# Two attention streams of one batch each become one stream of 16 head pairs, with a new preparation in front

## What is computed

```python
q = _split_heads(x @ Wq + bq, h)
k = _split_heads(x @ Wk + bk, h)
v = _split_heads(x @ Wv + bv, h)
pattern = jnp.einsum('bhid,bhjd->bhij', k, q) * scale
prob = jax.nn.softmax(pattern, axis=-2)
out = jnp.einsum('bhis,bhid->bhsd', prob, v)
concat = out.transpose(0, 2, 1, 3).reshape(b, s, h * dv)
return concat @ Wo + bo
```

## Time and profile before

| | us |
|---|---|
| median of 3 runs | 5114.24 (5112.64 to 5126.45) |
| the profiled execution, time | 5104.81 |
| its span | 5103.0 |
| mean granted clock of TensorE | 0.959 |

### The profile page before, as it was taken

How to read it: one execution, slowest core, us unless ns; L and a number is a source line. 1 busy time by engine, 2 the same in 40 slices (tenths; PEclk the granted TensorE clock), 3 DMA queues, 4 the chain that set the end, 5 groups by cost and what they waited for, 6 DMA issues and landing times.

```text
span 5103.0 us, 64759 instructions
## 1 busy us (share of the span) xinstructions
PE 4646.0 (91%) x21552; PEld 2817.8 (55%) x21552; DVE 3551.9 (70%) x4520; ACT 2193.0 (43%) x3447; POOL 2726.0 (53%) x1142
## 2 busy tenths in 40 slices
PE   5899999999999689999999999975989897999898
PEld 3455555555554245555555555534767675777576
DVE  4888888888786578878878778755556454556445
ACT  2344444444443234444444444333655443655442
POOL 0456656656666236666566566543666322666422
PEclk8899999999999789999999999997999998999898
DMA  1000000000000000000000000010000100000000
GB/s 41 5 4 2 5 4 2 5 4 2 5 1 2 20 5 4 2 6 1 5 6 1 6 5 1 2 37 17 1 1 1 35 1 17 1 1 1 0 1 33
DMA packets 57187, 37.21 MB, mean 7 GB/s; under 512 B 32972, under 2 KB 55456, under 8 KB 56864
## 3 DMA queue, kind: packets, MB, share of 16 engines
q1 hardware_dynamic: 56864, 33.02, 2.2%
HBM read 28.54 MB, written 4.19 MB: 6 GB/s over the span
## 4 chain that ended last, share of the span: by engine, by line
POOL 46%; issue 28%; PE 13%; DVE 8%; ACT 3%; POOLq 1%; DMA 1%; DVEq 0%; SPq 0%; ACTq 0%
POOL accp L639 35%; PE psum L1480 4%; POOL lp L661 4%; PE psum L1355 3%; POOL accp L635 3%; POOL rnorm L651 2%; POOL qk_u L656 2%; DVE ssq L1025 1%; ACT lp L785 1%; PE psum L1401 1%; DVE lnr L393 1%; ACT qk_sq L769 1%; PE psum L1493 1%; DVE lnc L398 1%; DVE qk_w L1037 1%
## 5 line engine op out<-in xcount | busy, mean ns | idle before, releaser
L639 POOL TENSOR_TENSOR accp<-accp,prob 128x1024 f32<-128x1024 f32 x640 | 1635.7, 2556 | 699.8 <-ACT prob L733 659.5
L733 ACT ACTIVATE prob<-psum 128x1024 f32<-128x1024 f32 x1024 | 1038.5, 1024 | 1669.5 <-PE psum L1258 1527.6
L922 DVE TENSOR_REDUCE mx<-psum 128x1 f32<-128x512 f32 x1920 | 1230.9, 683 | 382.6 <-PE psum L1235 351.0
L1269 PE MATMUL psum<-prob,vv 128*64 128x512 f32 x4096 | 991.9, 605 | 0.0
L1257 PE MATMUL psum<-qhh,klh 128*128 128x512 f32 x2048 | 837.3, 409 | 32.8 <-DVE klh L910 13.0
L1258 PE MATMUL psum<-qlm,kh 65*128 65x512 f32 x2048 | 823.7, 402 | 0.0
L1235 PE MATMUL psum<-klh,qhh 128*128 128x512 f32 x1920 | 699.8, 423 | 53.9 <-DVE mx L922 51.5
L1235 PEld LDWEIGHTS psum<-klh,qhh 128*128 128x128 f32 x1920 | 339.6, 191 | 448.8 <-DVE mx L922 309.7
L1269 PEld LDWEIGHTS psum<-prob,vv 128*64 128x64 f32 x4096 | 248.7, 136 | 509.9 <-issue 368.7
L1257 PEld LDWEIGHTS psum<-qhh,klh 128*128 128x128 f32 x2048 | 396.1, 193 | 211.7 <-issue 85.1
L639 POOL TENSOR_TENSOR accp<-prob 128x1024 f32<-128x1024 f32 x64 | 154.9, 2421 | 668.8 <-ACT prob L733 663.7
(11 more groups left out here) (152 smaller groups left out, 6725.2 us busy)
## 6 DMA issues: line engine op xcount, KB each, us to landing
tok<-L_attn_x SPq DMA_DIRECT2D x32, 128.0 KB, 2.2
rot_l<-const_rot SPq DMA_DIRECT2D x2, 2048.0 KB, 9.3
out<-lpT SPq DMA_DIRECT2D x32, 128.0 KB, 1.7
wqkv_l<-L_ffn_wqkv SPq DMA_DIRECT2D x4, 768.0 KB, 10.6
w_l<-L_ffn_w SPq DMA_DIRECT2D x4, 682.0 KB
wqk<-L_attn_Wq SPq DMA_DIRECT2D x32, 64.0 KB, 2.1
wqk<-L_attn_Wk SPq DMA_DIRECT2D x32, 64.0 KB, 2.2
wv_p<-L_attn_Wv SPq DMA_DIRECT2D x16, 128.0 KB, 2.3
```

Source lines behind the costliest of these rows:

```text
L639: pool.tensor_tensor(acc_p[cp][:], first[:], prob[kt % PRING][:], ALU.add).then_inc(pool_sum, 1)
L733: act.activation(prob[t % PRING][:], psum[:, S_BANK + 2 * (t % 2):S_BANK + 2 * (t % 2) + 2, :].rearrange("p a b -> p (a b)"), ACT.Exp, sca ...
L922: dve.tensor_reduce(mx4[:, j // CHUNKS, j % CHUNKS:j % CHUNKS + 1], ps, AX_X, ALU.max).then_inc(ring_free, 1)
L1269: mm = pe.matmul(psum[j * DH:(j + 1) * DH, O_BANK, :], vv[:, kt, s * DH:(s + 1) * DH], prob[t % PRING][:, j * T:(j + 1) * T], start=(kt == ...
```

## The change

The attention of both batches becomes one stream of 16 pairs (ALL_PAIRS). Pair 7 is the new BRIDGE: its heads carry maxima and projections of batch 1's first heads, and in groups 5 to 12 of its first head eight items turn_h. Each turns two token tiles of batch 1's normed input (four transposes) and VectorE writes them, scaled and shifted, over hT. The weights of the groups of turn_h in max_places become 3, those of groups 11 and 12 too. The six phases in front of layer norm 2 become one; pair 8 is a MIDDLE pair, written out on VectorE and SyncE and in the loop on TensorE.

Layer norm 1 works on token-major tiles, in quads of four: sum, centred squares, variance, power -0.5, one operation per tile; then the turn, and scale and shift at the read of PSUM. For batch 0, VectorE takes the sums and ScalarE the squares. For batch 1, ScalarE takes both (next_statistics) and GpSimd normalises into h_next, which the bridge reads.

The first head's maxima run in 32 couples of 512-column products. Between them stand on TensorE (ASIDE): from couple 1 on the second head's projections, the values, the bias product, and the 16 turns of the input into xT, read by ScalarE with gabo as bias. All loads of both batches' x are issued at the start, batch 1's behind the first weights and Wo.

```diff
-RING_PRO = V_ITEMS + RING_MAX + 1
+ALL_PAIRS = B * PAIRS
+COUPLES = RING_MAX // 2
+QUADS = KT // 4
+TWINS = KT // 2
+BRIDGE_PLACES = TWINS + 1
 ATT_SCALE = 1.0 / np.sqrt(np.float32(DH))
...
+        def quad(t):
+            return t[:].rearrange("p (t d) -> p t d", d=D)
+        x_quads = [[quad(t) for t in acc_p + acc_d],
+                   [x_tail[:, 4 * q:4 * q + 4, :] for q in range(3)] + [x_last[:]]]
+        h_quads = [[quad(t) for t in prob], [h_next[:, 4 * q:4 * q + 4, :] for q in range(QUADS)]]
+        wo_all = oT[:].rearrange("p (k n) -> p k n", n=D)
...
+            turns = range(TURN_GROUP, TURN_GROUP + TWINS) if which == BRIDGE and hh == 0 else ()
+            placed = max_places([*outs, *turns])
...
+        def places(kind, j, hh):
+            if kind == "turn":
+                return TURN_PLACES[hh]
+            if kind == "turn_h":
+                return 2 if j == TWINS - 1 else 1
...
+        ASIDE = {}
+        for n, item in enumerate([("qk", i) for i in range(QK_ITEMS)] + [("v", i) for i in range(V_ITEMS)]
+                                 + [("bo", i) for i in range(4)] + [("x", k) for k in range(2 * TWINS)]):
+            ASIDE.setdefault(1 + n, []).append(item)
+        P1_READ = (3, 4, 5, 6)
...
+            sp.dma_start(identf[:], eye).then_inc(id_in, 16)
+            for h in range(HALVES):
+                sp.dma_start(csil[:, h, :], c_in[:, h * P:(h + 1) * P].rearrange("b p -> p b")).then_inc(c_raw, 16)
+            sp.dma_start(wmod_sb, wmod.rearrange("(h p) n -> p h n", p=P)).then_inc(wm_in, 16)
+            for q in range(QUADS):
+                sp.dma_start(x_quads[0][q], x[0, q * T:(q + 1) * T, :].rearrange("(t p) d -> p t d", p=P)).then_inc(x0_in[q], 16)
...
+            load_head(0, 0)
+            load_head(1, 1)
+            load_wv(0)
+            sp.dma_start(bo_t[:], bo.rearrange("(m p) -> p m", p=P)).then_inc(bo_in, 16)
+            sp.dma_start(bv_t[:], bv.rearrange("(m p) -> p m", p=P)).then_inc(bo_in, 16)
+            sp.dma_start(wo_all, Wo.rearrange("(k p) n -> p k n", p=P)).then_inc(bo_in, 16)
+            for q in range(QUADS):
+                sp.dma_start(x_quads[1][q], x[1, q * T:(q + 1) * T, :].rearrange("(t p) d -> p t d", p=P)).then_inc(x1_in, 16)
             sp.sem_inc(mrow, 16)
-            for b in range(B):
...
+            pair(PAIRS - 1, False, PAIRS - 1, 0, BRIDGE)
+            pair(PAIRS, True, 0, 1, MIDDLE)
+            with sp.Fori(1, PAIRS - 1) as hp:
+                pair(hp + PAIRS, True, hp, hp + 1, MIDDLE)
+            pair(ALL_PAIRS - 1, True, PAIRS - 1, None, LAST)
...
+            for q in range(QUADS):
+                pool.wait_ge(var_ok, q + 1)
+                inverse_deviation(0, q)
+            for q in range(QUADS):
+                at = slice(4 * q, 4 * q + 4)
+                pool.wait_ge(sq1_ok, 4 * (q + 1))
+                pool.tensor_scalar(st_var[:, 1, at], st_ssq[:, 1, at], 1.0 / D, EPS, ALU.mult, ALU.add).then_inc(var1_ok, 1)
+                pool.wait_ge(var1_ok, q + 1)
+                inverse_deviation(1, q)
+                pool.wait_ge(rs1_ok, q + 1)
+                for t in range(4):
+                    i = 4 * q + t
+                    op = pool.tensor_scalar(h_quads[1][q][:, t, :], x_quads[1][q][:, t, :], st_neg[:, 1, i:i + 1], st_rs[:, 1, i:i + 1], ALU.add, ALU.mult)
+                op.then_inc(h1_ok, 1)
...
+            def next_statistics(q):
+                if q == 0:
+                    act.wait_ge(x1_in, 16 * QUADS)
+                for t in range(4):
+                    i = 4 * q + t
+                    if i >= 2:
+                        act.wait_ge(neg1_ok, i - 1)
+                    act.activation(copies[:, i % 2, :], x_quads[1][q][:, t, :], ACT.Copy, scale=-1.0 / D, accum_out=st_neg[:, 1, i:i + 1]).then_inc(neg1_ok, 1)
+                act.wait_ge(neg1_ok, 4 * (q + 1))
+                centred_squares(1, q)
...
+            def read_input(k):
+                act.wait_ge(xt_full, k + 1)
+                b, i = divmod(k, TWINS)
+                for h in range(HALVES):
+                    op = act.activation(xT[:, b, h, i * D:(i + 1) * D], psum[:, 1 + k % 3, h * D:(h + 1) * D], ACT.Identity, bias=gabo[:, b, h:h + 1])
+                op.then_inc(xt_ok, 1)
+            for q in range(QUADS):
+                act.wait_ge(neg_ok, q + 1)
+                centred_squares(0, q)
+            next_statistics(0)
+            next_statistics(1)
+            act.wait_ge(su_d, 3)
+            for q in range(QUADS):
+                act.wait_ge(ht_full, HALVES * q + 2)
+                act.activation(hT[:, 1, q * T:(q + 1) * T], psum[:, HALVES * (q % 2) + 1, :], ACT.Identity, bias=mod[:, 1, 0:1], scale=mod[:, 3, 0:1]).then_inc(ht_act, 1)
+            project(0, 0, 4)
+            project(1, 1)
+            for i in range(V_ITEMS):
+                act.wait_ge(vv_full, i + 1)
+                act.activation(vv[:, i * V_TILES:(i + 1) * V_TILES, :], psum[:, i, :].rearrange("p (t d) -> p t d", d=P), ACT.Copy).then_inc(vv_ok, 1)
+            act.wait_ge(gabo_ok, B)
+            for k in range(TWINS):
+                read_input(k)
+            next_statistics(2)
+            next_statistics(3)
+            for k in range(TWINS, 2 * TWINS):
+                read_input(k)
...
+            for q in range(QUADS):
+                means(q)
+            variances(0)
+            variances(1)
+            normal(0)
+            variances(2)
+            normal(1)
+            variances(3)
+            normal(2)
+            normal(3)
...
+            for q in range(QUADS):
+                dve.wait_ge(ht_full, HALVES * q + 1)
+                dve.tensor_scalar(hT[:, 0, q * T:(q + 1) * T], psum[:, HALVES * (q % 2), :], mod[:, 2, 0:1], mod[:, 0, 0:1], ALU.mult, ALU.add).then_inc(ht_dve, 1)
...
+            def out_bias():
+                dve.wait_ge(bo_full, 1)
+                dve.tensor_tensor(bo_all[:], psum[:, 0, 0:HALVES], bo_t[:], ALU.add).then_inc(su_d, 1)
+                dve.wait_ge(su_d, 8)
+                for b in range(B):
+                    dve.tensor_tensor(gabo[:, b, :], mod[:, 4:6, b:b + 1].rearrange("p k o -> p (k o)"), bo_all[:], ALU.mult).then_inc(gabo_ok, 1)
+            for i in range(QK_ITEMS):
+                proj_qk(0, 0, i, 4)
+            for k in range(COUPLES):
+                dve.wait_ge(pm_full, k + 1)
+                qt, c = divmod(2 * k, CHUNKS)
+                at = 4 + 2 * (k % 2)
+                dve.tensor_reduce(mx4[:, qt, c:c + 2], psum[:, at:at + 2, :], AX_X, ALU.max).then_inc(pm_free, 1)
+                if k in P1_READ:
+                    proj_qk(1, 1, P1_READ.index(k))
+                if k == BO_READ:
+                    out_bias()
+            dve.wait_ge(pm_free, COUPLES)
+            dve.tensor_reduce(mx1[:], mx4[:], AX_X, ALU.max).then_inc(mx_red, 1)
...
+            def next_hidden(rb, r, i, count):
+                ps = ring_wait(rb, r)
                 for h in range(HALVES):
...
+                    op = dve.tensor_scalar(hT[:, h, i * D:(i + 1) * D], ps[:, h * D:(h + 1) * D], mod[:, 2 + h, 1:2], mod[:, h, 1:2], ALU.mult, ALU.add)
+                op.then_inc(ring_free, count)
...
+            with dve.Fori(1, PAIRS - 1) as p:
+                pair(p, False, 0, MIDDLE)
+            pair(PAIRS - 1, False, 0, BRIDGE)
+            pair(PAIRS, True, 0, MIDDLE)
+            with dve.Fori(PAIRS + 1, ALL_PAIRS - 1) as p:
+                pair(p, True, 1, MIDDLE)
+            pair(ALL_PAIRS - 1, True, 1, LAST)
...
+            def turn_next(rb, r, i, count):
+                ring_slot(rb, r)
+                if i == 0:
+                    pe.wait_ge(h1_ok, QUADS)
+                turn_twin(M_BANK + r % RING, twin(h_quads[1], i)).then_inc(ring_full, count)
...
+            def first_maxima(k):
+                if k >= 2:
+                    pe.wait_ge(pm_free, k - 1)
+                qt, c = divmod(2 * k, CHUNKS)
+                for j in range(2):
+                    mm = pe.matmul(psum[:, 4 + 2 * (k % 2) + j, :], qhh[0][:, qt * P:(qt + 1) * P], klh[0][:, (c + j) * T:(c + j + 1) * T],
+                                   start=True, stop=True)
+                mm.then_inc(pm_full, 1)
...
+            def turn_input(k):
+                b, i = divmod(k, TWINS)
+                if k < 3:
+                    pe.wait_ge(vv_ok, k + 2)
+                else:
+                    pe.wait_ge(xt_ok, k - 2)
+                if k == TWINS:
+                    pe.wait_ge(x1_in, 16 * QUADS)
+                turn_twin(1 + k % 3, twin(x_quads[b], i)).then_inc(xt_full, 1)
+            for q in range(3):
+                turn_hidden(q)
+            hidden(0)
+            proj_qk(0, 0, 0, 1, 4)
+            turn_hidden(3)
+            for q in range(1, QUADS):
+                hidden(q)
+                proj_qk(0, 0, q, 1, 4)
+            projected(0, QK_ITEMS)
+            for k in range(COUPLES):
+                first_maxima(k)
+                for kind, j in ASIDE.get(k, ()):
```

(76 more changed lines are left out.)

654 lines of the change are left out of this document (305 added, 349 removed).

## The result

The changed kernel takes 4971.64 us (median of 4 runs, 4963.63 to 4978.41), before stands at 5116.68 beside it; the ratio is 0.9724, with a 95% interval of 0.9710 to 0.9739. Forecast were 4965 us, 4935 to 5005. The sum of the prediction was made for one profiled execution and gave 4955.8 us; that of the changed kernel took 4973.04 (span 4971.3), 17.2 more. So the size came out, but two errors of opposite sign lie in it: the start gained 13.5 us more than forecast, the stream of pairs 31.0 less.

What follows compares the result with a forecast made beforehand. TensorE was taken to set the pace of the pairs, with relays where no engine is full. Start 36.4 plus stream 112.6 gave 149.0 us off the 5114.2 median: 4965 us, range 4935 to 5005.

Steps and rivals of the forecast that it cites:

- Step 2: Start: ScalarE's sixteen squares with sums at 0.69 us each end at 22.8 us; transposes start at 26.5.
- Step 3: Start: ScalarE waits for batch 1's x until about 26 us, then 11.1 us of statistics to 37.1, delaying hT.
- Step 4: Start: turns, reads and first projection products alternate to about 44 us; projected at about 54.
- Step 5 and 6: Start: 32 couples of maxima, sum 58.8 us, plus an 8.9 us TensorE stall from ScalarE's statistics amid input reads.
- Step 7: Start: turn and store of the maxima 3.1 us as before; first scores at about 124.8 us.
- The rival of a cold preparation: Start: lower clock level holds through the new stage, first scores at 150, total 4990 us; chance 15%.
- The gap: Between the two batches' streams: batch 1's load, norm, projections and stand-alone maxima leave the path, 130.3 us removed.
- crowding: Bridge, groups 11 and 12: extra maxima and turn_h where VectorE has no room; 4 us TensorE stall, bounds 0 and 7.
- The seams: Pairs 8 and 9 after the bridge: 196.4 us (0 to 4.9 extra) and 199.3 us as first passes of loops.
- I count a boundary of VectorE's loops at 4 us: Where VectorE leaves a head-pair loop, the oT multiplications span 5.37 us against 1.39; 4 us added to pair 7.
- The rival "slower": Stream: first-pass price of 4.9 us at both heads of 15 pairs, 147 us; time say 5135 us; chance 2%.
- a disturbance: Batch 1's old stream: 1556.8 us measured against 1552.4 summed; 4.4 us that batch 0 lacks.

Runs made afterwards that it cites:

- the repeat: The changed kernel run once more with nothing edited: 4978.67 us, ratio 0.9731 to the kernel before.
- other places: Changed kernel with 73 or 32 empty instructions ahead of TensorE's first wait: 4955.67 us (ratio 0.9685) and 4975.8 us (0.9726).
- the fastest kernel: Changed kernel plus batch 1's statistics moved later, GpSimd's first addition per head waiting for VectorE's oT products, and 32 empty instructions: 4865.42 us, ratio 0.9507.
- GpSimd's wait: GpSimd's first addition of each head waits for VectorE's oT products of the head before: changed kernel 4917.5 us; kernel before, with it alone, 5047.3 us.

## Why the prediction came out

**The start** (forecast first scores at 124.8, measured 111.34). The order of the chain was right, and its sizes too large. Step 2: squares at 0.49 us, not 0.69; transposes at 23.5, not 26.5. Step 3: x of batch 1 landed at 27.6 (forecast 26), but statistics took 7.4 us, not 11.1. Step 4: projected at 51.8, not 54. Step 5 and 6: 56.9 us up to the turn of the maxima instead of 67.7, of which the stall is 4.95 instead of 8.9. The rest is in the couples: 3 to 6 took 9.2 us instead of 12.6, 7 to 12 took 11.7 instead of 13.5 (a part of the output bias 0.95 us instead of 1.7), 13 to 28 without the stall 19.4 instead of 22.4; those up to couple 2 gave some of it back, partly at the low clock. Step 7: 2.65 instead of 3.1. The 13.5 us are 2.2, 10.8 and 0.5. The late pieces that I named, ScalarE's half of hT and the input reads, were the ones; moving the statistics took these away. The rival of a cold preparation did not come: the maxima stage held a granted clock of 0.91.

**The gap** of 130.3 us went and did not come back: there is no stretch without scores between pair 7 and pair 8.

**The bridge** (forecast 206.8, measured 204.5, and 204.5 to 210.3 in the repeat and at other places). The transposes can be read directly. Each of the eight items takes 0.53 us of TensorE, up to the start of the next product, and one at the low clock 1.04; the eight sum to 4.75 us:

```profile
1538.28 0.60 PE L1348 MATMUL psum<-identf,h_next 128*128 128x128 f32 x4
1538.81 1.94 PE L1440 MATMUL psum<-prob,vv 128*64 128x512 f32 x8
```

With the fastest kernel the other terms can be estimated. A straight pair without collisions takes 190.9 us; a loop pair of before, 194.4, is that, one collision of 2.3 (194.4 against 192.1) and 1.2 for the turn. The bridge of the fastest kernel takes 197.5: transposes 4.7 (forecast 4.4) and crowding 1.9 (forecast 4). The 7.0 us up to 204.5 I put down to the two collisions; less the 2.3 and 1.2 that a loop pair has, 3.5 are left for the start (forecast 4). 194.4 + 4.7 + 1.9 + 3.5 = 204.5. Of these only the 4.7 is measured by itself: in three other kernels with GpSimd's wait the bridge took 199.5 to 200.8 us, with more of it at the low clock or one more wait of 1.1 us, so the split is good to 2 or 3 us. The page's rule that I weighed (the Trainium skill, "TensorE: Matmul & The Clock Gate", "Part 4: PE-mode transpose", 275 ns each) would, as an estimate, have made it 8.8 us for the transposes; the rows show 0.13 us each. On its other half, that transposes do not count as activity for the clock, no run here decides: the maxima stage held 0.91, but with products between the transposes.

**The seams.** Pair 8 was forecast at 196.4 and took 200.7: TensorE reaches its start without a turn, and the multiplications collided there too (5.61 us). Pair 9 was forecast at 199.3 and took 195.9: TensorE paused at the turn, so GpSimd came later and nothing collided. The step that failed here is "I count a boundary of VectorE's loops at 4 us". Its size was about right and its mechanism wrong: it is a collision of GpSimd's addition with VectorE's multiplications, and TensorE's pause at a loop's turn happens to avoid it. Hence the other reading that I missed: the 4.80 us and the wait of 2.62 us stood in the middle of every pair but the last of each stream, in the price of 194.4 us that I took as TensorE's own.

**The loop pairs** are the term that was mis-sized: "pairs 2 to 6 ... 972.0" took 996.4, and two of them, 200.9 and 201.4, passed the bound of 200 that I had set as a sign of being wrong. The same instructions cost 4.9 us a pair more, through a second pause of 1.25 us and the low clock behind it, since the loop lies at another place of TensorE's stream. The rival "slower" spoke of such a price at both heads of 15 pairs, 147 us; it came at one head of five pairs. The trace of before, with its one place, could not tell it; why one place brings a second pause stays open.

Pairs 10 to 13 took 6.0 us more than forecast: 12 and 13 took some 197.4 us each, with the granted clock at 0.50 for 3 to 7 us behind TensorE's 2.6 us waits in their middles, and in pair 12 also behind the turn. In the kernel before, two pairs of batch 1's loop took 197.7 and 197.5 us in just this way. They make the 4.4 us that the prediction called a disturbance and left out (6.2 in the loop, less 1.8 in the last pair); with GpSimd's wait in the kernel before, these two took 192.0 and 193.7. Why the clock falls behind these waits and not behind the others stays open.

So the forecast was right in its main mechanism, the gap and the relay at the start, and in its time, but partly because 13.5 us more gained at the start stand against 31.0 less in the stream; the terms of the stream add up as 24.4 (pairs 2 to 6), −2.3 (bridge), 4.3 and −3.4 (pairs 8 and 9), 7.7 (pairs 10 to 15) and 0.3 (pairs 0 and 1).

## What to carry to other kernels

When an instruction has two durations in one trace, look first at what the other engines do in the same microsecond, before giving the longer one to the control flow around it; here one wait on an engine with 10 us to spare was worth half as much as the whole rewrite. A pair's price "in its loop" can hold a stall in its middle: read the waits of one steady iteration too, not only those that distinguish it from the others. And a loop moved to another place of the same instruction stream may change its price by some 2%, so a forecast of a rewrite should carry that as a term, and two versions should be compared at more than one place.

## What the runs showed of the hardware

**GpSimd's additions hold up VectorE's multiplications.** Two products of 64x512 with both inputs in SBUF take 1.39 us alone and 4.8 to 5.6 us when a GpSimd addition of 128x1024 (2.38 us) has just begun and a second follows at once. At 1501 us in the changed kernel they began at 1501.22 and took 5.52; GpSimd's additions ran from 1501.05 to 1503.43 and from 1503.77 to 1506.19, and by my estimate 2 x 0.69 for the products and two blocked stretches, of 2.2 and some 2 us, make it up. Where the second addition comes later there is one such stretch, 3.2 to 3.8 us in all, at the first sum inside the heads (in all but one of them, the bridge's first, where GpSimd came late):

```profile
1465.12 3.23 DVE L1110 TENSOR_TENSOR oT<-o_raw,rcp 64x512 f32<-64x512 f32 x2
...
1464.71 2.38 POOL L709 TENSOR_TENSOR accp<-accp,prob 128x1024 f32<-128x1024 f32 x1 [0.75 <-ACT prob L848]
...
1467.94 2.63 POOL L709 TENSOR_TENSOR accp<-accp,prob 128x1024 f32<-128x1024 f32 x1 [0.85 <-ACT prob L848]
```

TensorE has no wait there, no maxima being placed in that group, and GpSimd's wait leaves these as they are. The Trainium skill, "SBUF — State Buffer", "Who interferes with whom", says that a VectorE instruction with two SBUF inputs contends with a GpSimd instruction that reads SBUF, and that the shared port pair is an exclusive lock; of VectorE's two-port modes it says that whoever issues first has the pair for its whole instruction and the other is blocked. The trace agrees, with these numbers, and shows the blocking for this plain multiplication too.

**A turn of a loop costs TensorE a pause of 1.0 to 1.8 us, or none, or two.** Pairs that aren't reached by a turn (1, 7, 8, 15) start without a pause. At the turns of the first loop, of the same instructions, there were two pauses 2.9 us apart, one, or none, with 0, 73 or 32 empty instructions ahead (with 32 in the fastest kernel none at four turns, and one of 3.1 us at the first). The Trainium skill, "Runtime: NRT & Kernel Launch", "Instruction fetch mechanics", says that instructions come in blocks and that a branch to one that isn't there has to wait for it. The pauses at turns fit that; what the distance to a block's edge does no run here measured, so the cause by way of fetching is argued and not shown. Shown is that the place alone makes the difference.

**The clock behind a pause.** In the changed kernel the first 14 us of pairs 2 to 6, behind two pauses, have a granted clock of 0.76 four times and 0.65 once. Behind the single pauses of the second loop (pairs 9 to 14) it is 1.00 five times and 0.88 once. So one pause of 1.1 to 1.5 us mostly left the clock alone here, and two of them, some 3 us apart, never did; what decides in the single case stays open.
